# Late weights split in short pieces, a norm's statistics on ScalarE, and redrawn orders of work: one Trainium2 core

## The chip, the cores and the metric

The kernel runs on one core of a Trainium2 chip (trn2). A core has TensorE (PE; its weight loads are listed apart as PEld), VectorE (DVE), ScalarE (ACT), GpSimd (POOL) and SyncE (SP), which issues the transfers here. Each engine runs its own instruction stream in order, and they meet only at semaphores. The metric is device time in microseconds (us) of one launch: 243.81 us is the median of three runs before the change (243.23 to 246.11).

## The reference, cut to what matters

`x` is (4, 256, 256): four batches of 256 tokens with 256 channels, a condition vector per batch, all in float32. Two layers follow each other. The first has an adaptive LayerNorm, attention over 16 heads of 16 channels, a projection, a second adaptive norm and a MLP of 1024 hidden units; the second has a norm by the root mean square, attention over four heads of 64 channels, an output projection and a skip.

```python
# layer 0; sc, sh and gm are six vectors of silu(cond) @ Wada.T + bada
a = ln(x) * (1 + sc1) + sh1            # ln: (x - m) / sqrt(var + 1e-6)
q, k, v = a @ Wqkv.T                   # q and k scaled to unit norm per head
x2 = x + gm1 * (softmax(q @ k.T + bias) @ v @ Wproj.T + bproj)
b = ln(x2) * (1 + sc2) + sh2
x3 = x2 + gm2 * (gelu(b @ Wfc1.T + bfc1) @ Wfc2.T + bfc2)
# layer 1
c = x3 * (scale * rsqrt(mean(x3 ** 2) + 1e-6))   # scale comes from cond
q, k, v = c @ qkv_w.T                  # unit norm times sqrt(scale), then rope
out = x3 + softmax(q @ k.T + mask) @ v @ out_w.T
```

The three norms are called kinds 0, 1 and 2 below: `ln(x)`, `ln(x2)` and the one by root mean square of `x3`.

## The kernel before, in words

**Orders written by hand.** The work is cut into steps with a name, a batch and a part (`fc1:2.1` is part 1 of `fc1` for batch 2). Five lists at the file's head, SYNC_ORDER, TENSOR_ORDER, VECTOR_ORDER, SCALAR_ORDER and POOL_ORDER, say in which order each engine walks its share of the steps; the same name in two lists is that step's work on two engines. Semaphores carry the data dependences, and nothing else sets the order.

**TensorE and its buffers.** Results go to three PSUM banks named `ring`, claimed in the order of TENSOR_ORDER; each must be emptied by VectorE or ScalarE before its next claim. The attention scores have two buffers `psx`, the value products `pv`. A float32 matmul is taken as three products of high and low halves (L835 to L837), so each operand, weight or tile, is split: the high half is a rounded copy, the low half the difference. `busy` steps (L974) are filler matmuls between the others, two per unit, 33 units. `normed` steps transpose a normalised tile (L841), `turn1` rotated q and k, `fc1` and `fc2` are the MLP, `qk1` and `v1` the second layer's projections, `max0` the scores from which VectorE takes row maxima (L1223), `score0` those that ScalarE exponentiates (L620).

**A norm** of a batch is a chain through the engines: the step `stats` on VectorE takes two variance statistics and two aggregates (L1188, L1190), then adds epsilon (L1192 for kinds 0 and 1; L1195 and L1196 for kind 2, where the squared mean is added to the variance as well); `stats` on GpSimd raises to the power −0.5 (L482); VectorE normalises two tiles (L1206); TensorE transposes them; ScalarE modulates (L607, L610); VectorE splits (L1215, L1216).

**The unit norms** of q and k: `square1` on ScalarE (L677; L670 in the first layer), sums and a seed on VectorE (`rsums1`, L1417 to L1183), three Newton rounds on GpSimd (`root1`, L490 to L493), rope and a product on VectorE (L1434 to L1443; in the first layer the product is L1356), then the transposes `turn1`.

**The late weights** w1, w2, wqkv1 and wout1 are loaded by SyncE (L446 to L458) into two staging areas, their high halves are taken by ScalarE (L591), their low halves by GpSimd in one instruction each (L546, L550, L554, L558). GpSimd also makes the additive mask (L515), the square roots of the second layer's scales (`key_scales`, L581 and L582), bias terms (`xbias0`, L533 and L534; `xbias1`, L540 and L542) and half of the rope (`cos`, L574). SyncE moves the row shifts of the first attention (`shift0`, L437).

After `fc2` VectorE forms x3 (L1405, L1408), from which the third norm starts. The GELU tiles are split by ScalarE (L746) and VectorE (L1397), the attention output by L1263.

## Time and profile before

| | |
|---|---|
| median of three runs | 243.81 us (243.23 to 246.11) |
| the profiled execution, its own time | 244.3 us |
| its span, first to last instruction | 242.4 us |
| TensorE busy; weight loads | 228.3 us (94%); 175.6 us (72%) |
| VectorE busy | 201.6 us (83%), 418 instructions |
| ScalarE busy | 156.6 us (65%), 316 instructions |
| GpSimd busy | 95.3 us (39%), 167 instructions |
| mean granted TensorE clock, as a share of the full one | 0.983 |

The profile is one execution. Its span is 1.9 us below its own time, and that time is 0.5 above the median of the runs. A busy share is an average over stages; matmuls overlap, so a group's "mean ns" is the latency of one and not the distance to the next. In a timeline row the first number is the start within the span, the second the time that the row's instructions took, and the bracket says how long the engine had been idle before and what it waited for.

### The profile page before, as it was taken

What the parts mean: (1) busy time and instruction counts of PE and PEld (TensorE: products, weight loads), DVE (VectorE), ACT (ScalarE), POOL (GpSimd) and SP (SyncE); (2) the same over time, 40 slices, a digit from 0 to 9 for tenths busy, and PEclk for the clock granted to TensorE, in tenths of its full rate; (3) what the DMA queues carried; (4) which work ended last, traced back from release to release, by engine and by line L of the source; (5) the groups of instructions that cost most, each with busy time, mean ns of one, the idle gap of its engine ahead of it and who ended that gap; (6) DMA issues with size and microseconds to landing.
All of it is one profiled execution on the core that took longest, in us unless ns stands there. A gap on an engine that the chain in (4) does not pass through costs nothing.

```text
span 242.4 us, 4991 instructions
## 1 busy us (share of the span) xinstructions
PE 228.3 (94%) x1792; PEld 175.6 (72%) x1792; DVE 201.6 (83%) x418; ACT 156.6 (65%) x316; POOL 95.3 (39%) x167
## 2 busy tenths in 40 slices
PE   6999999999999999999999999999999799998982
PEld 2679674575567758567689999999897476867762
DVE  3879889999996997997977998776898988998743
ACT  2430491854899987985989828753608695877930
POOL 7416317028203302380839194234505545550000
PEclk9797999999999999999999999999999999999998
DMA  6970040000000003203000100000000000000112
GB/s 209 329 302 3 1 173 1 3 1 5 3 0 9 0 3 96 85 0 105 34 3 0 47 0 0 3 0 3 0 0 4 0 0 1 3 0 0 47 43 92
DMA packets 3641, 9.75 MB, mean 40 GB/s; under 512 B 536, under 2 KB 920, under 8 KB 3360
## 3 DMA queue, kind: packets, MB, share of 16 engines
q1 hardware_dynamic: 3616, 9.41, 11.3%
q8 instruction: 16, 0.26, 0.4%
q14 instruction: 9, 0.07, 0.1%
HBM read 8.23 MB, written 1.05 MB: 38 GB/s over the span
## 4 chain that ended last, share of the span: by engine, by line
PE 65%; DVE 15%; ACT 6%; issue 5%; POOL 3%; DMA 3%; SPq 1%; POOLq 0%; ACTq 0%; DVEq 0%
PE ring L835 11%; PE ring L841 10%; PE ring L836 10%; PE ring L837 10%; PE pv L944 5%; DVE nm L1223 5%; PE psx L974 5%; PE ring L898 3%; PE pv L1133 2%; PE psx L924 2%; DVE qn L1356 2%; DMA stage_a<-in_wada 2%; PE ring L848 1%; PE psx L1105 1%; DVE qstk L1397 1%
## 5 line engine op out<-in xcount | busy, mean ns | idle before, releaser
L1223 DVE TENSOR_REDUCE nm<-ring 128x2 f32<-128x512 f32 x64 | 40.2, 684 | 1.3 <-PE ring L898 0.8
L620 ACT ACTIVATE ps<-psx 128x1024 f32<-128x1024 f32 x32 | 31.4, 1026 | 6.0 <-PE psx L924 5.9
L835 PE MATMUL ring<-wqkv_hi,xm_hi 128*128 128x512 f32 (+1 forms) x64 | 24.2, 379 | 0.2
L974 PE MATMUL psx<-ident_b 128*128 128x512 bf16 x66 | 21.4, 449 | 2.0 <-POOL ones L477 2.0
L836 PE MATMUL ring<-wqkv_lo,xm_hi 128*128 128x512 f32 (+1 forms) x64 | 22.0, 343 | 0.0
L837 PE MATMUL ring<-wqkv_hi,xm_lo 128*128 128x512 f32 (+1 forms) x64 | 22.0, 343 | 0.0
L898 PE MATMUL ring<-kstk,qstk 64*128 64x256 f32 x128 | 19.4, 327 | 1.9 <-DVE nm L1223 1.6
L734 ACT ACTIVATE ps<-ring,col 128x256 f32<-128x256 f32 x32 | 13.3, 476 | 11.8 <-PE ring L837 11.2
L898 PEld LDWEIGHTS ring<-kstk,qstk 64*128 64x128 f32 x128 | 12.3, 184 | 10.5 <-DVE nm L1223 5.9
L490 POOL TENSOR_TENSOR nt<-ss,rn 128x64 f32<-128x64 f32 (+1 forms) x24 | 7.1, 296 | 32.3 <-DVE rn L1183 31.1
L574 POOL TENSOR_TENSOR stage_a<-qk,rope_sb 128x512 f32<-128x512 f32 x8 | 11.3, 1408 | 19.9 <-ACT qk L757 19.8
L835 PE MATMUL ring<-xm_hi,w_sb 128*128 128x256 f32 x64 | 18.5, 289 | 0.0
L836 PE MATMUL ring<-xm_lo,w_sb 128*128 128x256 f32 x64 | 18.1, 282 | 0.0
L837 PE MATMUL ring<-xm_hi,w_sb 128*128 128x256 f32 x64 | 18.1, 282 | 0.0
L944 PE MATMUL pv<-ps,vs 128*32 128x256 f32 x256 | 16.9, 385 | 0.0
L841 PE MATMUL ring<-ident,stack 128*128 128x128 f32 x128 | 16.0, 276 | 0.0
L841 PEld LDWEIGHTS ring<-ident,stack 128*128 128x128 f32 x128 | 14.2, 141 | 2.0 <-DVE nm L1223 0.4
L783 ACT ACTIVATE ps<-psx,nm 128x256 f32<-128x256 f32 x32 | 14.8, 484 | 1.1 <-DVE nm L1450 1.1
L542 POOL TENSOR_TENSOR xs<-x,stage_a 128x512 f32<-128x512 f32 x4 | 5.5, 1384 | 24.5 <-DVE x L1390 24.4
L482 POOL TENSOR_TENSOR rstd<-ve,half_neg 128x2 f32<-128x2 f32 x12 | 10.1, 844 | 12.2 <-DVE ve L1192 9.5
L835 PEld LDWEIGHTS ring<-wqkv_hi,xm_hi 128*128 128x128 f32 x64 | 12.6, 197 | 3.1 <-issue 0.7
L924 PE MATMUL psx<-qstk,kstk 64*128 64x256 f32 x128 | 13.6, 304 | 0.5 <-DMA qstk<-stage_a 0.2
(198 smaller groups left out, 680.2 us busy)
## 6 DMA issues: line engine op xcount, KB each, us to landing
stage_a<-in_wada SPq DMA_DIRECT2D x3, 512.0 KB, 8.5
xs<-in_x SPq DMA_DIRECT2D x4, 256.0 KB, 7.4
stage_a<-in_wfc SPq DMA_DIRECT2D x1, 1024.0 KB, 4.8
stage_b<-in_wfc SPq DMA_DIRECT2D x1, 1024.0 KB, 4.7
out<-x SPq DMA_DIRECT2D x4, 256.0 KB, 2.0
stage_b<-in_wqkv SPq DMA_DIRECT2D x1, 768.0 KB, 6.1
stage_a<-in_wqkv SPq DMA_DIRECT2D x1, 768.0 KB, 4.3
row<-in_rows SPq DMA_DIRECT2D x1, 394.0 KB, 8.0
```

Source lines behind the costliest of these rows:

```text
L620: a.activation(ps[:, n % 4], psx[:, n % 2], ACT.Exp).then_inc(exp_done, 1)
L734: last = a.activation(gelu_u[:, n % 4, i * L:(i + 1) * L], bank(key)[:, i * L:(i + 1) * L], ACT.Gelu_apprx_tanh, bias=col[:, 16 + 2 * i_ + ...
L783: ins = a.activation(weights_q[m % 2][:, i, f, :], psx[:, n % 2, i, f, :], ACT.Exp, bias=nm1[:, m % 2, 2 * i + f:2 * i + f + 1], accum_out ...
L835: mm(dst, lhs[0], rhs[0], start=start, stop=False)
L836: mm(dst, lhs[0], rhs[1], start=False, stop=False)
L837: return mm(dst, lhs[1], rhs[0], start=False, stop=stop)
L841: last = nc.tensor.transpose(dst[:, i * P:(i + 1) * P], src, ident[:, :])
L898: last = mm(dst[par][:, qc * L:(qc + 1) * L], qstk[rows_, b % 2, p, qc * P:(qc + 1) * P], kstk[rows_, b % 2, p, :], start=True, stop=not w ...
L924: last = mm(dst[:, i, kc, :], kstk[head_rows(i), b % 2, p, keys], qstk[head_rows(i), b % 2, p, :], start=True, stop=not with_bias)
L944: last = mm(pv[32 * i:32 * i + 32, cols_], vs[:, b % 3, kc, 4 * g + i, :], ps[:, slot, i % 2, kc, :], start=(kc == 0), stop=(kc == TB - 1))
L974: mm(psx[:, 0, 0], ident_b[:, :], ident_b[:, :].unsqueeze(1).to_broadcast([P, 4, P]), start=True, stop=True)
L1223: v.tensor_reduce(nm[:, :, par, p], bank(key).rearrange("p (q n) -> p q n", q=TB), AX.X, ALU.max, negate=True).then_inc(ring_dve, 1)
```

## The change

Four things change.

1. A function `take_lo` on GpSimd makes the low half of a late weight in pieces of 512 columns (4, 4, 3 and 1 of them) where one instruction did it. Only the last piece signals.
2. For kinds 0 and 1 VectorE no longer adds epsilon. `rstd_of` on GpSimd does it in an instruction of its own ahead of the power.
3. For kind 2 VectorE has no `stats2` step. ScalarE squares each of the batch's two tiles of x3 and sums it in the same instruction, each waiting for the one before; GpSimd multiplies the sum by 1/256 and adds epsilon.
4. The five lists are redrawn. SyncE issues w1's load behind the first row shift and w2's behind the fourth. GpSimd makes the key scales later and the bias term `xbias1:3` behind `root1:0`. TensorE keeps its 33 filler units, one more of them ahead of `ada`.

The file is longer by some lines, so line numbers differ: the statistics' squares are L696, the modulation L620, the q and k copy L778, the turned copy L793, the pieces L507, epsilon L487 and L490, the power L491.

On GpSimd, after the third batch's inverse root of the first attention (`rn` is the root, `sqs` the key scales), before and after:

```order
L493 TENSOR_TENSOR rn<-rn,nt 128x64
L524 TENSOR_TENSOR rn<-rn,sm 128x2x16
L581 TENSOR_TENSOR sqs<-row,half_pos 128x4
L582 TENSOR_TENSOR sqs<-row,half_pos 128x4
L515 TENSOR_SCALAR mask_add<-o_tok 128x2048
```

```order
L501 TENSOR_SCALAR nt<-nt 128x64
L502 TENSOR_TENSOR rn<-rn,nt 128x64
L539 TENSOR_TENSOR rn<-rn,sm 128x2x16
L530 TENSOR_SCALAR mask_add<-o_tok 128x2048
L499 TENSOR_TENSOR nt<-ss,rn 128x64
```

The two powers are gone from here, so the mask follows the root at once. In the same engine's stretch around the second MLP weight (`kstk` holds its low half), first before and then after:

```order
L540 TENSOR_TENSOR stage_a<-gam,row 128x256
L542 TENSOR_TENSOR xs<-x,stage_a 128x512
L533 TENSOR_TENSOR stage_a<-gam,row 128x256
L534 TENSOR_TENSOR xs<-xs,stage_a 128x512
L550 TENSOR_TENSOR kstk<-stage_b,kstk 128x2048
L482 TENSOR_TENSOR rstd<-ve,half_neg 128x2
L554 TENSOR_TENSOR wqkv_lo<-stage_a,wqkv_hi 128x1536
```

```order
L594 TENSOR_TENSOR sqs<-row,half_pos 128x4
L595 TENSOR_TENSOR sqs<-row,half_pos 128x4
L548 TENSOR_TENSOR stage_a<-gam,row 128x256
L549 TENSOR_TENSOR xs<-xs,stage_a 128x512
L507 TENSOR_TENSOR kstk<-stage_b,kstk 128x512 x4
L487 TENSOR_SCALAR ve<-mv 128x2
L491 TENSOR_TENSOR rstd<-ve,half_neg 128x2
L487 TENSOR_SCALAR ve<-mv 128x2
L491 TENSOR_TENSOR rstd<-ve,half_neg 128x2
L507 TENSOR_TENSOR wqkv_lo<-stage_a,wqkv_hi 128x512 x3
```

The key scales left the place ahead of the mask and stand ahead of w2's split; two norms' epsilon and power now come between the two splits, where one power stood.

On ScalarE, where the fourth batch's `fc2` ends and the second layer's attention begins (`junk` is the squares' unused output, `gam` and `vs` hold turned and value tiles), before and after:

```order
L762 ACTIVATE vs<-ring 128x2x256
L607 ACTIVATE xmt<-ring,mod 128x256 x4
L757 ACTIVATE qk<-ring 128x512
L772 ACTIVATE gam<-ring 128x4x128
L677 ACTIVATE qn<-qk 128x512
L757 ACTIVATE qk<-ring 128x512
L772 ACTIVATE gam<-ring 128x4x128
L677 ACTIVATE qn<-qk 128x512
```

```order
L783 ACTIVATE vs<-ring 128x2x256
L696 ACTIVATE junk,mv<-xs 128x256 x2
L620 ACTIVATE xmt<-ring,mod 128x256 x2
L793 ACTIVATE gam<-ring 128x4x128
L620 ACTIVATE xmt<-ring,mod 128x256 x2
L696 ACTIVATE junk,mv<-xs 128x256 x2
L793 ACTIVATE gam<-ring 128x4x128
L778 ACTIVATE qk<-ring 128x512
L690 ACTIVATE qn<-qk 128x512
L778 ACTIVATE qk<-ring 128x512
L690 ACTIVATE qn<-qk 128x512
```

The two pairs of squares are `stats2:2` and `stats2:3`. The second pair stands ahead of the second turned tile and of the next tile's copy and square.

The diff, with the lists of TensorE, VectorE and ScalarE cut to the head and the passage from the fourth batch's `fc2` on:

```diff
--- before.py
+++ after.py
@@ -67,6 +67,7 @@
 R_END = 1300
 R_KZERO = C
 FILL = 2
+PIECE = 512
 
 
 
@@ -81,80 +82,81 @@
 
 
 SYNC_ORDER = steps("""
-load_w1 shift0:0 shift0:1 shift0:2 load_w2 shift0:3 load_wqkv1 load_wout1 proj1:0 proj1:1 proj1:2 proj1:3
+shift0:0 load_w1 shift0:1 shift0:2 shift0:3 load_w2 load_wqkv1 load_wout1 proj1:0 proj1:1 proj1:2 proj1:3
 """)
 
 TENSOR_ORDER = steps("""
-busy:0 busy:1 busy:2 busy:3 busy:4 ada normed0:0 busy:5 busy:6 busy:7 busy:8 busy:9 busy:10 busy:11 qk0:0.0
...
-normed1:1 score0:3.6 score0:3.7 out0:3.0 proj0:2 value0:3.2 value0:3.3 fc1:0.0 fc1:0.1 fc1:0.2 out0:3.1 fc1:0.3
-heads0:3 fc1:1.0 fc1:1.1 proj0:3 normed1:2 fc1:1.2 fc2:0 fc1:1.3 fc1:2.0 fc1:2.1 normed1:3 fc1:2.2 fc1:2.3
-normed2:0 fc2:1 qk1:0.0 fc1:3.0 qk1:0.1 fc1:3.1 fc2:2 fc1:3.2 fc1:3.3 v1:0 normed2:1 fc2:3 normed2:2 qk1:1.0
...
+busy:0 busy:1 busy:2 busy:3 busy:4 busy:5 ada busy:6 normed0:0 busy:7 busy:8 busy:9 busy:10 busy:11 busy:12
...
+out0:3.1 fc1:0.3 heads0:3 fc1:1.0 fc1:1.1 fc1:1.2 proj0:3 fc1:1.3 normed1:2 fc2:0 fc1:2.0 fc1:2.1 fc1:2.2
+normed1:3 fc1:2.3 normed2:0 fc2:1 qk1:0.0 qk1:0.1 fc1:3.0 fc1:3.1 fc1:3.2 fc1:3.3 fc2:2 v1:0 normed2:1 turn1:0.0
+fc2:3 normed2:2 turn1:0.1 qk1:1.0 qk1:1.1 score1:0.0 score1:0.1 v1:1 normed2:3 qk1:2.0 qk1:2.1 v1:2 turn1:1.0
...
 score1:3.0 turnp1:2.1 turninv1:2 score1:3.1 value1:2 turnp1:3.0 proj1:1 turnp1:3.1 turninv1:3 value1:3 proj1:2
 proj1:3
 """)
 
 VECTOR_ORDER = steps("""
...
 unit0:3.1 v0:2 max0:2.4 max0:2.5 max0:2.6 lo0:3.0 max0:2.7 neg0:2 heads0_lo:0 lo0:3.1 shift0:2 proj0:0 stats1:0
 out0:1.0 max0:3.0 max0:3.1 max0:3.2 norm1:0 max0:3.3 max0:3.4 max0:3.5 out0:1.1 max0:3.6 max0:3.7 neg0:3
...
-fc2:1 stats2:1 gelu:2.3 gelu:3.0 rsums1:0 norm2:1 gelu:3.1 fc2:2 stats2:2 gelu:3.2 gelu:3.3 rope:0.0 split2:1
-norm2:2 rope:0.1 fc2:3 split2:2 stats2:3 rsums1:1 max1:0.0 norm2:3 max1:0.1 rope:1.0 rope:1.1 inv1:0.0 split2:3
-inv1:0.1 rsums1:2 max1:1.0 turnp1:0.0 turnp1:0.1 rope:2.0 rope:2.1 inv1:1.0 max1:1.1 rsums1:3 turnp1:1.0
...
+rsums1:0 norm2:1 gelu:2.3 gelu:3.0 gelu:3.1 gelu:3.2 rope:0.0 fc2:2 gelu:3.3 split2:1 rope:0.1 norm2:2 fc2:3
+split2:2 norm2:3 rsums1:1 max1:0.0 max1:0.1 rope:1.0 rope:1.1 split2:3 inv1:0.0 inv1:0.1 turnp1:0.0 rsums1:2
+turnp1:0.1 max1:1.0 rope:2.0 rope:2.1 heads1_scaled:0 inv1:1.0 max1:1.1 rsums1:3 max1:2.0 inv1:1.1 turnp1:1.0
...
 """)
 
 SCALAR_ORDER = steps("""
...
-gelu:3.0 gelu:3.1 fc1:3.2 gelu:3.2 fc1:3.3 gelu:3.3 v1:0 normed2:1 normed2:2 qk1:1.0 turn1:0.0 square1:1.0
-qk1:1.1 turn1:0.1 square1:1.1 v1:1 exp1:0.0 normed2:3 qk1:2.0 exp1:0.1 turn1:1.0 qk1:2.1 v1:2 turn1:1.1
...
+gelu:3.0 gelu:3.1 fc1:3.2 gelu:3.2 fc1:3.3 gelu:3.3 v1:0 stats2:2 normed2:1 turn1:0.0 normed2:2 stats2:3
+turn1:0.1 qk1:1.0 square1:1.0 qk1:1.1 square1:1.1 exp1:0.0 v1:1 normed2:3 exp1:0.1 qk1:2.0 qk1:2.1 v1:2
...
 """)
 
 POOL_ORDER = steps("""
-const_stack const_v stats0:0 const_sel stats0:1 stats0:2 root0:0 stats0:3 xbias0:0 root0:1 root0:2 key_scales
-mask root0:3 xbias1:0 xbias0:1 stats1:0 split_w1 xbias1:1 stats1:1 xbias0:2 xbias1:2 xbias0:3 split_w2 stats1:2
-split_wqkv1 xbias1:3 stats1:3 stats2:0 split_wout1 cos:0.0 cos:0.1 stats2:1 root1:0 stats2:2 cos:1.0 cos:1.1
-stats2:3 root1:1 cos:2.0 cos:2.1 root1:2 cos:3.0 cos:3.1 root1:3
+const_v const_sel stats0:0 stats0:1 stats0:2 root0:0 stats0:3 const_stack xbias0:0 root0:1 root0:2 mask root0:3
+stats1:0 xbias1:0 xbias0:1 split_w1 xbias1:1 stats1:1 xbias0:2 xbias1:2 key_scales xbias0:3 split_w2 stats1:2
+stats1:3 split_wqkv1 stats2:0 split_wout1 cos:0.0 cos:0.1 stats2:1 root1:0 xbias1:3 stats2:2 stats2:3 cos:1.0
+cos:1.1 root1:1 cos:2.0 cos:2.1 root1:2 cos:3.0 cos:3.1 root1:3
 """)
 
 BRANCH = TENSOR_ORDER.index(("branch",))
@@ -238,7 +240,8 @@
 
 def build(nc, x, wqkv, wproj, wada, wfc1, wfc2, wnorm, wqkv1, wout1, cols, rows, rope, bias, mask, out):
     ring_plan = Ring(TENSOR_ORDER)
-    stat_no = positions(VECTOR_ORDER, ["stats0", "stats1", "stats2"])
+    stat_no = positions(VECTOR_ORDER, ["stats0", "stats1"])
+    rstd_no = positions(POOL_ORDER, ["stats0", "stats1", "stats2"])
     norm_keys = [key[1:] for key in ring_plan.keys if key[0] == "xT"]
     norm_no = {key: n for n, key in enumerate(norm_keys)}
 
@@ -292,6 +295,7 @@
         mv = sb("mv", [P, 3, B, TB, 2])
         ve = sb("ve", [P, 3, B, TB])
         rstd = sb("rstd", [P, 3, B, TB])
+        junk = sb("junk", [P, C])
         zero_col = sb("zero_col", [P, 1])
         ss = sb("ss", [P, TB, 2 * H0])
         rn = sb("rn", [P, TB, 2 * H0])
@@ -358,7 +362,7 @@
         w_hi, w_lo_d, w_lo_p = sem("weights_hi"), sem("weights_lo_vector"), sem("weights_lo_pool")
         xb_ready = sem("x_bias_ready")
         x2_ready, x2b_ready, x3_ready = sem("x2_ready"), sem("x2_bias_ready"), sem("x3_ready")
-        stats_ready, rstd_ready = sem("stats_ready"), sem("rstd_ready")
+        stats_ready, rstd_ready, squares_summed = sem("stats_ready"), sem("rstd_ready"), sem("squares_summed")
         xh_ready, xmt_ready, xm_ready = sem("xh_ready"), sem("xmt_ready"), sem("xm_ready")
         sq_ready, seed_ready, rn_ready = sem("sq_ready"), sem("seed_ready"), sem("rn_ready")
         qn_ready, stk_hi, stk_lo = sem("qn_ready"), sem("stack_hi"), sem("stack_lo")
@@ -478,7 +482,12 @@
             g.memset(row[:, R_KZERO:R_KZERO + C], 0.0).then_inc(kbias_zero, 1)
 
             def rstd_of(kind, b):
-                pool.wait_ge(stats_ready, stat_no[(kind, b)] + 1)
+                if kind < 2:
+                    pool.wait_ge(stats_ready, stat_no[(kind, b)] + 1)
+                    step(g.tensor_scalar(ve[:, kind, b, :], mv[:, kind, b, :, 1], LN_EPS, None, ALU.add))
+                else:
+                    pool.wait_ge(squares_summed, TB * (b + 1))
+                    step(g.tensor_scalar(ve[:, kind, b, :], mv[:, kind, b, :, 1], 1.0 / C, LN_EPS, ALU.mult, ALU.add))
                 g.tensor_tensor(rstd[:, kind, b, :], ve[:, kind, b, :], half_neg[:, 0:TB], ALU.pow)\
                  .then_inc(rstd_ready, 1)
 
@@ -491,6 +500,12 @@
                     step(g.tensor_tensor(t, t, y, ALU.mult))
                     step(g.tensor_scalar(t, t, -0.5, 1.5, ALU.mult, ALU.add))
                     step(g.tensor_tensor(y, y, t, ALU.mult))
+
+            def take_lo(lo, whole, hi):
+
+                for n in range(0, whole.shape[1], PIECE):
+                    ins = g.tensor_tensor(lo[:, n:n + PIECE], whole[:, n:n + PIECE], hi[:, n:n + PIECE], ALU.subtract)
+                ins.then_inc(w_lo_p, 1)
 
             for step_ in POOL_ORDER:
                 name, b = step_[0], step_[1] if len(step_) > 1 else None
@@ -543,20 +558,18 @@
                                     ALU.add).then_inc(x2b_ready, 1)
                 if name == "split_w1":
                     pool.wait_ge(w_hi, 4)
-                    g.tensor_tensor(w1_lo, stage_a[:, 0:FC * HID].rearrange("p (f n) -> p f n", f=FC),
-                                    w1_hi, ALU.subtract).then_inc(w_lo_p, 1)
+                    take_lo(w1_sb[:, 1, :], stage_a[:, 0:FC * HID], w1_sb[:, 0, :])
                 if name == "split_w2":
                     pool.wait_ge(w_hi, 5)
-                    g.tensor_tensor(w2_lo, stage_b[:, :].rearrange("p (f n) -> p f n", f=HC),
-                                    w2_hi, ALU.subtract).then_inc(w_lo_p, 1)
+                    take_lo(w2_lo.rearrange("p f n -> p (f n)"), stage_b[:, :], w2_hi.rearrange("p f n -> p (f n)"))
                 if name == "split_wqkv1":
                     pool.wait_ge(w_hi, 6)
-                    g.tensor_tensor(wqkv_lo[:, :, :], stage_a[:, 0:FC * 3 * C].rearrange("p (f n) -> p f n", f=FC),
-                                    wqkv_hi[:, :, :], ALU.subtract).then_inc(w_lo_p, 1)
+                    take_lo(wqkv_lo[:, :, :].rearrange("p f n -> p (f n)"), stage_a[:, 0:FC * 3 * C],
+                            wqkv_hi[:, :, :].rearrange("p f n -> p (f n)"))
                 if name == "split_wout1":
                     pool.wait_ge(w_hi, 7)
-                    g.tensor_tensor(wo_lo[:, :, :], stage_b[:, 0:FC * C].rearrange("p (f n) -> p f n", f=FC),
-                                    wo_hi[:, :, :], ALU.subtract).then_inc(w_lo_p, 1)
+                    take_lo(wo_lo[:, :, :].rearrange("p f n -> p (f n)"), stage_b[:, 0:FC * C],
+                            wo_hi[:, :, :].rearrange("p f n -> p (f n)"))
                 if name == "root1":
                     inverse_root(seed1_ready, b, 2 * H1)
                     g.tensor_tensor(rn[:, :, 0:2 * H1], rn[:, :, 0:2 * H1],
@@ -675,6 +688,14 @@
                         act.wait_ge(*full(("T1", t - TB)))
                     act.wait_ge(*emptied(("qk1", t)))
                     a.activation(qn[:, t % TB, :], qk[:, t % TB, :], ACT.Square).then_inc(sq1_ready, 1)
+                if name == "stats2":
+                    act.wait_ge(x3_ready, b + 1)
+                    for i in range(TB):
+                        if b or i:
+                            act.wait_ge(squares_summed, TB * b + i)
+                        a.activation(junk[:, :], xs[:, TB * b + i, :], ACT.Square,
+                                           accum_out=mv[:, 2, b, i, 1:2])\
+                         .then_inc(squares_summed, 1)
                 if name == "hi0":
 
                     t = TB * b + i_
@@ -1187,18 +1208,14 @@
                 for i in range(TB):
                     step(v.bn_stats(bnst[:, kind, b, i, :], src[:, TB * b + i, :]))
                 for i in range(TB):
-                    step(v.bn_aggr(mv[:, kind, b, i, :], bnst[:, kind, b, i, :]))
-                if kind < 2:
-                    v.tensor_scalar(ve[:, kind, b, :], mv[:, kind, b, :, 1], LN_EPS, None, ALU.add).then_inc(stats_ready, 1)
-                else:
-
-                    step(v.tensor_tensor(ve[:, kind, b, :], mv[:, kind, b, :, 0], mv[:, kind, b, :, 0], ALU.mult))
-                    v.scalar_tensor_tensor(ve[:, kind, b, :], ve[:, kind, b, :], LN_EPS, mv[:, kind, b, :, 1],
-                                           ALU.add, ALU.add).then_inc(stats_ready, 1)
+                    last = v.bn_aggr(mv[:, kind, b, i, :], bnst[:, kind, b, i, :])
+                    if i == 0:
+                        step(last)
+                last.then_inc(stats_ready, 1)
 
             def normalise(kind, b, src):
                 n = norm_no[(kind, b)]
-                dve.wait_ge(rstd_ready, stat_no[(kind, b)] + 1)
+                dve.wait_ge(rstd_ready, rstd_no[(kind, b)] + 1)
                 if n >= 1:
                     dve.wait_ge(*full(("xT",) + norm_at[n - 1]))
                 for i in range(TB):
@@ -1406,9 +1423,6 @@
                      .then_inc(ring_dve, 1)
                     dve.wait_ge(*emptied(("f2", b)))
                     v.tensor_tensor(xs[:, batch, :], x2[:, batch, :], xs[:, batch, :], ALU.add).then_inc(x3_ready, 1)
-                if name == "stats2":
-                    dve.wait_ge(x3_ready, b + 1)
-                    statistics(2, b, xs)
                 if name == "rsums1":
                     if b >= 1:
                         dve.wait_ge(rn1_ready, b)
```

## Rows read from the trace of the kernel before

**Rows 1.** Stretches: from:to, length, busy of PE, PEld, DVE, ACT, POOL, clock, DMA, GB/s.

```profile
135.00:175.00 40.00, 39.36 (x317) 38.64 (x317) 32.58 (x66) 24.06 (x51) 18.48 (x23) 1.00 0.01 5
...
190.00:219.50 29.50, 27.59 (x192) 20.56 (x192) 26.51 (x51) 22.56 (x67) 14.68 (x35) 1.00 0.00 1
```

**Rows 2.** Waits of TensorE, whole span: engine, buffer, line, releaser: us, times, longest.

```profile
PE ring L841 <- DVE qn L1443: 1.8, 2, 1.2
PE ring L898 <- DVE nm L1223: 1.6, 6, 0.4
...
PE ring L835 <- DVE stack L1397: 0.5, 1, 0.5
```

**Rows 3.** Timeline, 58 to 64 us: start, us, engine, line, operation; idle before.

```profile
58.22 1.03 POOL L581 TENSOR_TENSOR sqs<-row,half_pos 128x4 f32<-128x4 f32 x1
...
58.80 0.68 DVE L1356 TENSOR_TENSOR qn<-qk,rn 128x512 f32<-128x512 f32 x1
...
60.44 1.90 POOL L515 TENSOR_SCALAR mask_add<-o_tok 128x2048 bf16<-128x2048 uint8 x1
60.60 2.27 DVE L1356 TENSOR_TENSOR qn<-qk,rn 128x512 f32<-128x512 f32 x1
```

**Rows 4.** Timeline, 125 to 138 us: w2's split and the GELU low parts.

```profile
128.69 4.60 POOL L550 TENSOR_TENSOR kstk<-stage_b,kstk 128x2048 fp32r<-128x2048 f32 x1
...
131.06 3.38 DVE L1397 TENSOR_TENSOR qstk<-ps,qstk 128x512 fp32r<-128x512 f32 x2 [0.17 <-ACT qstk L746]
...
135.10 0.38 PE L835 MATMUL ring<-wp_hi,at_hi 128*128 128x256 f32 x1 [0.30 <-DVE at_lo L1263]
```

**Rows 5.** Timeline, 139.5 to 143.3 us: the split of wqkv1 and an epsilon.

```profile
139.75 3.52 POOL L554 TENSOR_TENSOR wqkv_lo<-stage_a,wqkv_hi 128x1536 fp32r<-128x1536 f32 x1 [5.34 <-ACT wqkv_hi L591]
...
140.94 2.35 DVE L1192 TENSOR_SCALAR ve<-mv 128x2 f32<-128x2 f32 x1
```

**Rows 6.** Timeline, 180 to 194 us: x3, statistics, squares and the rope wait.

```profile
181.11 0.47 PE L835 MATMUL ring<-wqkv_hi,xm_hi 128*128 128x512 f32 x1
...
181.68 0.69 DVE L1408 TENSOR_TENSOR xs<-x,xs 128x512 f32<-128x512 f32 x1
...
182.58 0.60 PE L841 MATMUL ring<-ident,qn 128*128 128x128 f32 x4
...
183.35 0.88 DVE L1188 BATCH_NORM_STATS2 bnst<-xs 128x6 f32<-128x256 f32 x2
...
183.80 0.63 ACT L677 ACTIVATE qn<-qk 128x512 f32<-128x512 f32 x1
...
184.90 0.16 DVE L1196 SCALAR_TENSOR_TENSOR ve<-ve,mv 128x2 f32<-128x2 f32 x1
...
193.19 0.66 PE L841 MATMUL ring<-ident,qn 128*128 128x128 f32 x4 [1.17 <-DVE qn L1443]
```

**Rows 7.** Groups of VectorE: line, shapes, count; busy us, mean ns; idle before.

```profile
L1192 DVE TENSOR_SCALAR ve<-mv 128x2 f32<-128x2 f32 x8 | 4.2, 520 | 0.3
```

**Rows 8.** Groups of GpSimd: additions, the power, a Newton step, wout1's split.

```profile
L482 POOL TENSOR_TENSOR rstd<-ve,half_neg 128x2 f32<-128x2 f32 x12 | 10.1, 844 | 12.2 <-DVE ve L1192 9.5 <-DVE ve L1196 2.8
...
L534 POOL TENSOR_TENSOR xs<-xs,stage_a 128x512 f32<-128x512 f32 x4 | 5.1, 1282 | 0.3
...
L492 POOL TENSOR_SCALAR nt<-nt 128x16 f32<-128x16 f32 x12 | 3.2, 270 | 1.0
...
L558 POOL TENSOR_TENSOR wo_lo<-stage_b,wo_hi 128x512 fp32r<-128x512 f32 x1 | 1.8, 1822 | 5.1 <-ACT wo_hi L591 5.1
```

**Rows 9.** Groups of ScalarE: the exponential with sum and its read-out.

```profile
L783 ACT ACTIVATE ps<-psx,nm 128x256 f32<-128x256 f32 x32 | 14.8, 484 | 1.1 <-DVE nm L1450 1.1
...
L783 ACT ACTIVATION_READ_ACCUMULATOR ps<-psx,nm 128x1 f32 x32 | 6.9, 217 | 0.0
```

**Rows 10.** Timeline of SyncE, 30 to 140 us, and the page's transfer of w2.

```profile
110.61 1.27 SPq L437 DMA_DIRECT2D qstk<-stage_a  x2
...
stage_b<-in_wfc SPq DMA_DIRECT2D x1, 1024.0 KB, 4.7
```

89 lines of the change are left out of this document (45 added, 44 removed).

## The prediction

> **What bounds the kernel now.** Read the stretches first [rows 1]. From 135 to 175 us TensorE is busy 39.36 of 40.00 us at the full clock: in that stretch nothing that another engine does can shorten the run by more than 0.6 us. From 190 to 219.5 it is busy 27.59 of 29.50. So the question is not how busy VectorE is, but which of TensorE's few waits goes and which new one comes. The table of waits comes second [rows 2]: VectorE's rope product 1.8 us in two pieces, its row maxima of the first attention 1.6 in six, one GELU low part 0.5. VectorE's and GpSimd's work costs time only where it reaches such a wait.
>
> Third, the timeline, for what makes VectorE late. A VectorE instruction that meets a long GpSimd instruction lasts until that one ends. The unit-norm product takes 2.27 us beside the mask, against 0.68 just before [rows 3]; two GELU low parts take 3.38 beside the 4.60 us split of the second MLP weight [rows 4]; an addition of two columns takes 2.35, from 140.94 to 143.29, inside a split that ends at 143.27 [rows 5]. Over their usual lengths (0.68 each, and 0.16 for an operation on two columns, [rows 6]) that is 1.59 + 2.02 + 2.19 = 5.8 us.
>
> **The change part by part.**
>
> *Epsilon to GpSimd.* Eight VectorE additions go, 4.2 us of busy time [rows 7], of which 2.9 is more than the 0.16 that each needs. On GpSimd each becomes an instruction of about 270 ns in front of the power (the nearest row has 16 columns, [rows 8]): +0.1 us on a norm's chain, in all eight chains 0.8, all beside other work but the first at the head. I take 0, up to +0.2. The Trainium skill, "GPSIMD Engine Reference", section "When to use GPSIMD", gives plain elementwise work to VectorE as the faster engine, which speaks against this move; 270 against 160 ns agrees.
>
> *Weights in pieces.* The four splits have 2048, 2048, 1536 and 512 columns and now run as 4 + 4 + 3 + 1 pieces. The nearest row for a piece with two full inputs is GpSimd's 128x512 addition, 1282 ns; the upper one is the split that has 512 columns already, 1822 [rows 8]. Four pieces last 5.1 us by the first and 7.3 by the second, against 4.60 in one instruction; I take 5.1, which lies nearer to the 4.60. VectorE's longest wait shrinks towards one piece; the sum of its waiting need not. The Trainium skill, "SBUF — State Buffer", says in its section on who interferes with whom that VectorE and GpSimd hold a shared port for a whole instruction. The trace agrees: the 2.35 us addition ended with the split. By that rule alone the pieces would give 0 where four VectorE instructions follow each other. The place where it reaches TensorE is the 0.30 wait for a projection's low part at 135.10, behind the 3.38 us pair [rows 4]; I count that wait below, with the lists, and the pieces themselves 0.
>
> On the other side stands the w2 split's start. The key-scale powers, from 58.22 to 60.44 [rows 3], moved ahead of it: 128.69 + 2.2 = 130.9. With pieces of 1.28 it ends at 136.0, with 1.82 at 138.2. Behind it on GpSimd is the next norm's epsilon and power (0.27 + 0.84, [rows 8]), then VectorE normalises two tiles of 256 columns, 0.7 if each takes half of the 0.68 that 512 take: the tile is there at 137.8 or at 140.0. TensorE wanted it one projection unit after 135.10. Such a unit is twelve products of 256 columns, and six of 512 took 182.58 − 181.11 = 1.47 [rows 6], so at 136.6; two further `fc1` units of that length now come first: 139.5. So 1.7 us to spare, or 0.5 late: 0, up to +0.5. The split of wqkv1 now waits behind the fourth batch's epsilon too, whose projection moved one `fc1` unit back; it ended at 143.27 [rows 5], and between the tile at 139.5 and `qk1:0.0` TensorE has two `fc2` and five `fc1` units, 7.4 us by the latter alone: 0.
>
> *Third norm to ScalarE.* VectorE loses four times 1.71 us (183.35 to 185.06, [rows 6]), 6.8 us. ScalarE gets eight squares of 256 columns with a summed output. The nearest rows are its exponential of that width with sum: 484 ns, and 217 for the read-out [rows 9]. I take 0.65 each because every square waits for the one before; 0.48 and 0.70 are the ends. That is 1.3 per batch (0.97 to 1.4), 5.2 in all. Batches 0 to 2 stand in stretches with room, ScalarE 24.06 busy of 40 [rows 1]: 0. Batch 3 is the place to watch, in the rivals.
>
> *Mask and key scales.* The mask moves 2.2 us ahead, to 58.2, where VectorE runs maxima rather than the product that was held for 1.59. Since TensorE waits for those maxima 0.4 at most at a time [rows 2], I take −0.4, between 0 and −1.5.
>
> *Loads.* w2's load goes to behind the fourth shift (110.61 + 1.27 = 111.9) and lands 4.7 us later [rows 10], 12 us before GpSimd's split of it: 0. Without that cover the split and the 0.5 us margin behind it would go at once. w1's load, behind the first shift, has more room still.
>
> *Redrawn lists.* TensorE keeps its 33 filler units. At the head one more stands before the conditioning products, and the first data come by DMA either way: −0.2 (−0.2 to 0). ScalarE squares the second batch's last q and k tile ahead of a copy of about 0.6 instead of behind it, and a root on GpSimd follows: −0.4 (−0.6 to 0). The six maxima waits lose some in the stretch to 135: −0.2 (−1.0 to 0). The GELU wait of 0.5 before `fc2:3` [rows 2]: TensorE now has the four transposes of `turn1:0.0` first, 0.6 by the row at 182.58 [rows 6], while VectorE splits the last GELU tile later, behind `fc2:2`. With the 0.30 of 135.10: −0.5 together (−0.8 to +0.4). At 193.19 TensorE waits 1.17 for the rope product; ahead of that transpose stand now two more units, `qk1:2.1` and `v1:2`, of 1.47 each. All of it would go, less what batch 3's squares take from the same chain: −0.6 (−1.17 to +1.3).
>
> Sum: 0 + 0 + 0 − 0.4 − 0.2 − 0.4 − 0.2 − 0.5 − 0.6 = −2.3. The profiled execution took 244.3, so 242.0; the median of the runs shown, 243.81, lies 0.5 under it: **241.5 us**.
>
> **The rivals.**
> *ScalarE becomes the wait (slower).* `stats2:3` must wait for the sum x3, which VectorE ends at 182.37, and stands now ahead of a copy of turned tiles, the next tile's copy and its square; that square began at 183.80 [rows 6]. Now it can begin at 182.37 + 1.3 + two copies of 0.6 = 184.9, 1.1 later, and root, rope and the transpose of 193.19 follow. If the three ring banks hold back the two units meant as cover, the 1.17 wait grows to 2.3 while the other terms give nothing: 243.8 + 1.1 to 1.3 = 245.0, and 245.7 with the 0.5 and 0.2 above. It decides from the point where the square begins over 2.4 us after x3 (1.4 before) and the wait at this transpose stays above 1. For it: ScalarE executes in order. Against: VectorE, which held the chain as well, is 1.7 us freer at just this place.
>
> *Nothing moves.* TensorE is dense, and each removed wait is followed by another as long: 243.8, within 1 us. For it: 39.36 of 40.
>
> *VectorE was the bound all along (faster).* 11 us of its work go and up to 5.8 of port waits could follow. If all that the bounds name goes (0.2 + 0.6 + 1.5 + 1.0 + 0.8 + 1.17 = 5.3), the time is 238.5. For it: the large waits of TensorE are all for VectorE [rows 2]. Against: they are spread over a dozen places, and behind each stands a TensorE with other work.
>
> **How the numbers follow.** Forecast, a gain of 1 to 4.9: 0.57. Nothing moves: 0.21. ScalarE's wait, or another that ends above 244.8: 0.12. VectorE the bound: 0.10. Two per cent is 4.9 us, which is about what a measurement of this kernel, its three runs 2.9 us apart, tells from no change. Under 238.9 lie the last rival and a little of the forecast: faster 0.12. Over 248.7 lies only a loss in a place not named here: 0.04. The range goes from 238.5, that rival's value, to 245.4, within the slow rival's; the forecast's own is 239.5 to 243.
>
> **What would show it.** VectorE's busy sum some 11 us lower, ScalarE's 5 higher; no VectorE instruction held for over 1.5 us beside a split; the unit-norm product at 0.68 everywhere; the rope wait of TensorE gone in the stretch from 185; the last squares' successor within 2.4 us of x3. Wrong if TensorE's total waiting stays as it was, if pieces cost 1.8 us each, or if TensorE waits for the tile behind the w2 split.

## The result: slower by 1.25 %, and the profile after

The changed kernel took 248.06 us (median of 19 runs, 244.93 to 249.58) against 243.75 for the kernel before (median of 19); the ratio is 1.0125 with a 95% interval of 1.0094 to 1.0157. The ratio leaves out the four longest of the 19 runs as slow ones, so it is smaller than the 4.3 us (1.8%) between the medians. The prediction was 241.5. The runs of the changed kernel stand in two groups: eight have spans of 243.1 to 244.9 us and ten of 246.2 to 247.7, with one between. The kernel before has two levels as well, 16 runs of 242.5 to 244.6 us and three of 246.0 to 246.7; front_only below shows that they are another matter. The profile shown first is of the lower group, 245.02 us with a span of 243.2; a second profile of the same kernel, `after_again`, is of the upper one, span 246.8.

The page after, lower group: busy times, and TensorE's granted clock in 40 slices.

```profile
PE 228.3 (94%) x1792; PEld 174.5 (72%) x1792; DVE 193.6 (80%) x386; ACT 160.2 (66%) x332; POOL 100.5 (41%) x187
...
PEclk9999999999999999999999999999999989999999
```

VectorE lost 8 us of busy time instead of the 11 forecast, ScalarE gained 3.6 instead of 5, and GpSimd gained 5. TensorE's work is the same to 0.1 us. So the result is once more a matter of its waits. The table of them answers to [rows 2] (engine, buffer, line, releaser: us in total, times, longest):

```profile
PE ring L862 <- ACT qk L778: 1.9, 1, 1.9
...
PE ring L856 <- ACT vs L783: 1.4, 1, 1.4
PE ring L919 <- DVE nm L1240: 1.3, 4, 0.4
PE ring L856 <- ACT ps L755: 0.8, 1, 0.8
PE ring L856 <- DVE at_lo L1280: 0.6, 1, 0.6
```

Of the three waits of before, rope's 1.8 and the GELU part's 0.5 are gone as table entries, and the maxima's 1.6 fell to 1.3. In their place TensorE waits 1.9, 1.4 and 0.8 for **ScalarE to empty a ring bank**, for which it had not waited over 0.2 us before. The stretches that answer to [rows 1]:

```profile
135.00:175.00 40.00, 39.20 (x314) 38.16 (x313) 27.30 (x48) 24.18 (x58) 20.03 (x30) 1.00 0.02 7
190.00:219.50 29.50, 26.19 (x176) 18.98 (x176) 24.12 (x47) 21.58 (x64) 14.17 (x36) 0.94 0.01 2
```

From 135 to 175 VectorE has 5.3 us less to do than before and TensorE is no busier. From 190 to 219.5 TensorE is busy 1.4 us less, and the granted clock was 0.94 on average, where the profile before has 1.00 in that stretch.

Three sums of TensorE's waits (those over 0.05 us) tell where the time came and went; later kernels are put beside them. The last row is the kernel of load_order, the changed one but for two loads, whose profile (span 246.2) is of the upper group too.

| profile | 30 to 124 us | 124 to 183 (MLP) | 183 to 223 (second layer) | granted 1.2 GHz for 3.4 us at |
|---|---|---|---|---|
| before | 3.23 | 0.83 | 2.33 | 8.9, 19.1 |
| changed, lower group | 2.56 | 1.42 | 3.31 | 198.4 |
| changed, upper group | 2.53 | 3.93 | 3.33 | 146.6, 201.2 |
| load_order, upper group | 2.51 | 3.00 | 4.44 | 146.7 |

**The second layer.** The timeline of the changed kernel (start, us, engine; the bracket says how long the engine was idle and for whom), which answers to [rows 6]:

```profile
183.22 2.55 POOL L587 TENSOR_TENSOR stage_a<-qk,rope_sb 128x512 f32<-128x512 f32 x2
...
183.27 2.65 DVE L1223 TENSOR_SCALAR xh<-xs,zero_col,rstd 128x256 f32<-128x256 f32 x2 [1.12 <-POOL rstd L491]
...
185.84 1.26 DVE L1431 TENSOR_REDUCE ss<-qn 128x8 f32<-128x512 f32 x2
...
191.36 0.50 PE L856 MATMUL ring<-wqkv_hi,xm_hi 128*128 128x512 f32 x1 [1.36 <-ACT vs L783]
...
192.48 0.69 DVE L1457 TENSOR_TENSOR qn<-qn,rn 128x512 f32<-128x512 f32 x1 [1.08 <-POOL rn L575]
...
194.43 1.27 POOL L587 TENSOR_TENSOR stage_a<-qk,rope_sb 128x512 f32<-128x512 f32 x1 [2.05 <-ACT qk L778]
...
194.60 1.64 DVE L1457 TENSOR_TENSOR qn<-qn,rn 128x512 f32<-128x512 f32 x1
...
196.28 0.60 ACT L778 ACTIVATE qk<-ring 128x512 f32<-128x512 f32 x1 [1.92 <-DVE qn L1457]
...
197.02 0.63 PE L862 MATMUL ring<-ident,qn 128*128 128x128 f32 x4 [1.89 <-ACT qk L778]
```

VectorE's two normalising operations meet the two `cos` products of GpSimd and take 2.65 us instead of 0.74 before. Two moves bring them together: GpSimd's list now has that norm's power (`stats2:3`) ahead of the `cos` pair instead of behind it, and VectorE's list has the normalising pair ahead of the row sums. So the row sums start at 185.84, although their squares were ready at 185.07. The root (`rn`), which before ended while VectorE had other work, now ends so late that VectorE itself waits for it (1.08 before the product at 192.48). TensorE cannot use `qk1:2.1` and `v1:2` freely as cover meanwhile. `qk1:2.1` itself waits 1.36 us, because the ring bank of `v1:1` is not emptied: ScalarE has that behind `exp1:0.0`. Then the transpose `turn1:1.1` needs the bank of `qk1:2.1`, whose copy overwrites a buffer that rope must have read. That copy waits 1.92 for the rope product (itself held to 1.64 us by the next `cos`), and TensorE waits 1.89 for the copy.

**The MLP, upper group.** The timeline of `after_again`:

```profile
140.71 1.71 DVE L1223 TENSOR_SCALAR xh<-x,mv,rstd 128x256 f32<-128x256 f32 x2 [0.61 <-POOL rstd L491]
...
140.83 4.12 POOL L507 TENSOR_TENSOR wqkv_lo<-stage_a,wqkv_hi 128x512 fp32r<-128x512 f32 x3 [0.15 <-ACT wqkv_hi L604]
...
142.34 1.49 DVE L1232 CAST xm_hi<-xmt 128x512 fp32r<-128x512 f32 x1
...
143.87 1.63 DVE L1233 TENSOR_TENSOR xm_lo<-xmt,xm_hi 128x512 fp32r<-128x512 f32 x1
...
145.56 0.39 PE L856 MATMUL ring<-xm_hi,w_sb 128*128 128x256 f32 x1 [2.63 <-DVE xm_lo L1233]
```

and of the lower group at the same place:

```profile
141.11 0.42 DVE L1232 CAST xm_hi<-xmt 128x512 fp32r<-128x512 f32 x1
...
141.56 0.69 DVE L1233 TENSOR_TENSOR xm_lo<-xmt,xm_hi 128x512 fp32r<-128x512 f32 x1
...
142.03 4.78 POOL L507 TENSOR_TENSOR wqkv_lo<-stage_a,wqkv_hi 128x512 fp32r<-128x512 f32 x3 [1.61 <-ACT wqkv_hi L604]
```

In the profile of the upper group the three pieces of wqkv1's split and three VectorE instructions in a row take turns: the second normalising operation, the cast and the low part are held to 1.71 (for two), 1.49 and 1.63 us, and the tile that `fc1:2.0` needs is there at 145.5 instead of 142.25. TensorE waits 2.63 us. In the profile of the lower group GpSimd comes to that split 1.2 us later, when the chain is through. The profiles of load_order and turn_order, both of the upper group, show the same: the split at 140.9 and TensorE's wait of 2.63 or 2.64. Behind this wait the clock falls (stretch, length, busy of PE, PEld, DVE, ACT, POOL, granted clock, DMA):

```profile
143.20:146.60 3.40, 1.04 (x8) 1.05 (x9) 3.37 (x4) 0.00 (x0) 1.75 (x2) 1.00 0.00 0
146.60:150.01 3.41, 3.41 (x18) 3.41 (x17) 1.40 (x3) 1.74 (x6) 0.36 (x2) 0.50 0.00 0
150.01:153.40 3.39, 3.39 (x31) 3.39 (x30) 0.74 (x2) 2.58 (x7) 0.53 (x1) 1.00 0.00 0
```

TensorE was busy 1.04 of 3.40 us, and for the next 3.41 us it was granted 1.2 GHz instead of 2.4: 18 matmuls came where the stretch behind has 31. In the profile of the lower group such a stretch stands in the second layer, behind the 1.36 and 1.89 us waits:

```profile
194.90:198.38 3.48, 1.59 (x15) 1.26 (x12) 2.52 (x5) 2.10 (x5) 2.23 (x2) 1.00 0.01 2
198.38:201.79 3.41, 3.41 (x14) 1.74 (x13) 2.40 (x6) 1.78 (x4) 0.50 (x3) 0.50 0.00 0
```

How much each costs can be read by matching TensorE's matmuls one by one, load_order's profile against that of the lower group. It is 0.4 us ahead up to this wait, 2.5 behind right after it, 3.7 behind at the end of the stretch at 1.2 GHz, and 2.6 behind from 149.5 us on, where the lower group waits 0.78 for ScalarE. So the wait makes 2.9 us of the 3.1 between the groups, and of the 1.2 that the stretch costs about 1.0 comes back.

The Trainium skill, "SBUF — State Buffer", section on who interferes with whom, has it that the engine that issues first holds the shared port for its whole instruction. The alternation above agrees: each of VectorE's three instructions gives way to one piece of 1.3 to 1.5 us.

### The profile page after: what moved, and what is told of

Its sections match the earlier page's. It is cut to its first block, busy times and chain, and to the rows that moved or that the text cites. A ratio compares the mean times of both kernels' runs of the same rounds, so it can differ in the third digit from the quotient of the medians.

```text
span 243.2 us, 4998 instructions
## 1 busy us (share of the span) xinstructions
PE 228.3 (94%) x1792; PEld 174.5 (72%) x1792; DVE 193.6 (80%) x386; ACT 160.2 (66%) x332; POOL 100.5 (41%) x187
## 4 chain that ended last, share of the span: by engine, by line
PE 65%; DVE 19%; POOL 5%; issue 5%; ACT 3%; DMA 1%; SPq 0%; ACTq 0%; POOLq 0%; DVEq 0%
PE ring L862 13%; PE ring L856 9%; PE ring L858 7%; PE ring L857 7%; PE pv L965 5%; PE psx L995 5%; DVE nm L1240 5%; PE ring L919 4%; PE psx L945 3%; PE pv L1154 3%; PE psx L1126 3%; DVE qstk L1414 2%; DVE xh L1223 1%; DVE stack L1414 1%; DVE bnst L1209 1%
## 5 line engine op out<-in xcount | busy, mean ns | idle before, releaser
L856 PE MATMUL ring<-wqkv_hi,xm_hi 128*128 128x512 f32 (+1 forms) x64 | 23.5, 368 | 1.4 <-ACT vs L783 1.4
L995 PE MATMUL psx<-ident_b 128*128 128x512 bf16 x66 | 20.0, 427 | 2.0 <-POOL ones L481 2.0
L858 PE MATMUL ring<-wqkv_hi,xm_lo 128*128 128x512 f32 (+1 forms) x64 | 21.5, 337 | 0.0
L919 PE MATMUL ring<-kstk,qstk 64*128 64x256 f32 x128 | 18.4, 322 | 1.3 <-DVE nm L1240 1.3
L587 POOL TENSOR_TENSOR stage_a<-qk,rope_sb 128x512 f32<-128x512 f32 x8 | 10.4, 1313 | 14.1 <-ACT qk L778 14.1
L856 PEld LDWEIGHTS ring<-wqkv_hi,xm_hi 128*128 128x128 f32 x64 | 12.1, 189 | 5.1 <-ACT vs L783 1.8
L487 POOL TENSOR_SCALAR ve<-mv 128x2 f32<-128x2 f32 x8 | 2.9, 366 | 28.6 <-DVE mv L1211 28.3
L856 PEld LDWEIGHTS ring<-xm_hi,w_sb 128*128 128x128 f32 x64 | 12.2, 191 | 1.7 <-ACT ps L755 1.0
```

What stands on the lines that cost most here:

```text
L856: mm(dst, lhs[0], rhs[0], start=start, stop=False)
L858: return mm(dst, lhs[1], rhs[0], start=False, stop=stop)
L919: last = mm(dst[par][:, qc * L:(qc + 1) * L], qstk[rows_, b % 2, p, qc * P:(qc + 1) * P], kstk[rows_, b % 2, p, :], start=True, stop=not w ...
L995: mm(psx[:, 0, 0], ident_b[:, :], ident_b[:, :].unsqueeze(1).to_broadcast([P, 4, P]), start=True, stop=True)
```

## The experiments

Ratios are to the kernel before, run on the same chip, with a 95% interval. The chips differ from one set of runs to another, so kernels are compared by their ratios first.

**after_again**, no edit. 

> The changed kernel once more, nothing altered. Its 19 runs fell into two groups, spans of 243.1 to 244.0 us and of 246.2 to 247.7, at the same granted clock (0.992 and 0.993 in both groups). Theory 'two levels': again both groups occur, 3 us apart, and a trace of the higher one shows one place with 3 us more. Rival 'spread': spans fill the range between 243 and 247 evenly and no single place holds the difference.

247.09 us, 1.0124 (1.0073 to 1.0176). Five spans of 243.0 to 244.9, one of 245.7, four of 246.2 to 246.8. All three traces of the upper group (this one, load_order, turn_order) have the surplus at one place, above: 'two levels' holds in the main. This one has another 1.1 us at a GELU wait of 0.94 at 177 us, which the other two lack.

**turn_order**, TensorE and ScalarE:

```diff
-... v1:1 normed2:3 qk1:2.0 qk1:2.1 v1:2 turn1:1.0 ...
+... v1:1 normed2:3 qk1:2.0 turn1:1.0 qk1:2.1 v1:2 ...      # TensorE
-... exp1:0.0 v1:1 normed2:3 exp1:0.1 qk1:2.0 qk1:2.1 v1:2 turn1:1.0 ...
+... v1:1 exp1:0.0 normed2:3 exp1:0.1 qk1:2.0 turn1:1.0 qk1:2.1 v1:2 ...   # ScalarE
```

> The changed kernel, but turn1:1.0 stands ahead of qk1:2.1 and v1:2 again on TensorE and ScalarE, and v1:1 ahead of exp1:0.0 on ScalarE. Theory 'ring banks': in the changed kernel TensorE waits 1.36 us at 191.4 for ScalarE to empty v1:1 and 1.89 at 197.0 for the copy of qk1:2.1, which itself waits for rope; before, the waits of this place were 0.48, 1.17 and 0.61. So these two fall from 3.25 to about 1.7 and the span is 1 to 1.6 us shorter than the changed kernel's. Rival 'the rope chain decides': the 2.65 us of the two normalising operations beside the cos pair keep the root late, the waits only move to turn1:1.0, and the time stays within 0.5 us.

247.69 us, 1.0133 (1.0039 to 1.0228): nothing gained. The two waits became one of 3.22 us for rope:

```profile
185.93 2.66 DVE L1222 TENSOR_SCALAR xh<-xs,zero_col,rstd 128x256 f32<-128x256 f32 x2 [1.11 <-POOL rstd L490]
...
195.90 0.66 PE L861 MATMUL ring<-ident,qn 128*128 128x128 f32 x4 [3.22 <-DVE qn L1456]
```

The 2.66 us of the normalising pair beside `cos` are there as in the changed kernel, and between 183 and 223 us TensorE waits 4.59 us, against 4.44 in load_order's profile of the same group. So the rival holds: the banks decide on which instruction TensorE waits, the rope chain decides how long.

**load_order**, SyncE's list of before:

```diff
-shift0:0 load_w1 shift0:1 shift0:2 shift0:3 load_w2 ...
+load_w1 shift0:0 shift0:1 shift0:2 load_w2 shift0:3 ...
```

> The changed kernel with SyncE's order of before: w1's load ahead of the first row shift, w2's ahead of the fourth. Theory 'loads collide': the higher group of runs comes from the 1 MB loads that now follow the row shifts directly; the higher group disappears or is as rare as before (3 runs of 19). Rival 'loads are hidden': 12 us of cover, so both groups stay as frequent and the lower group stays at 243.1 to 244.0 us of span.

248.01 us, 1.0122 (1.0003 to 1.0241), three of four runs at 246.2 us of span or more and one at 243.3: both groups stay. Four runs can't tell how often each comes, but the loads are not what makes the upper one.

**code_only**: the three code parts with the lists of before (stats2 from VectorE's list to ScalarE's). 

> The kernel before with the three code parts of the change (pieces of 512, epsilon on GpSimd, squares on ScalarE), the lists of before, stats2 being moved to ScalarE's list at the same places and left out of VectorE's. Theory 'the redrawn lists cost it': the code parts alone are worth 0 to -1 us against before (243.4). Rival 'the parts cost it': pieces with 1.28 to 1.8 us each, epsilon on GpSimd and ScalarE's squares are themselves 1 to 3 us slower.

244.82 us, 1.0057 (1.0012 to 1.0101), 1.4 us slower: inside the rival's 1 to 3, and somewhat under half of the 3.0 by which the ratio puts the changed kernel behind. Three more kernels took one part each, in the lists of before.

**pieces_only**: `PIECE = 512` and `take_lo`. 

> The kernel before with pieces of 512 columns alone. code_only, with all three code parts, took 1.4 us more than before. Theory 'pieces': 3 pieces last 4.1 us against 3.5, 4 last up to 6.5 against 4.6 where VectorE takes turns with them; the norm behind comes later, +0.4 to +1.0 us. Rival 'pieces are neutral or good': the low part for the projection at 135 waits less, TensorE's waits at 148 and 152 don't appear, -0.3 to +0.2.

243.58 us, 0.9970 (0.9933 to 1.0007): no change that the ratio can tell. But nine of the 35 runs of the kernel before stood on its higher level here and one of these 14. Among the lower spans alone the medians are 241.05 before and 241.6 with pieces, half a microsecond longer; front_parts below bears this out.

**eps_only**:

```diff
+                if kind < 2:                                                    # GpSimd
+                    step(g.tensor_scalar(ve[:, kind, b, :], mv[:, kind, b, :, 1], LN_EPS, None, ALU.add))
...
-                    v.tensor_scalar(ve[:, kind, b, :], mv[:, kind, b, :, 1], LN_EPS, None, ALU.add).then_inc(stats_ready, 1)
+                    last.then_inc(stats_ready, 1)                               # VectorE
```

> The kernel before with the epsilon addition of the first two norms on GpSimd, nothing else. Theory 'chain': the addition on GpSimd takes 0.2 to 0.57 us against 0.17 on VectorE, in chains that are mostly covered: 0 to +0.3. Rival 'eps costs it': TensorE waits at the normed tiles near 134, 148 and 152, as in code_only (0.45, 0.40, 0.22): +0.6 to +1.0.

242.95 us, 0.9988 (0.9951 to 1.0026): neutral. In the changed kernel an epsilon took 366 ns in the mean against the 270 forecast, and w2's four pieces 6.0 us against 5.1 (line, shapes, count; busy us, mean ns; idle before):

```profile
L507 POOL TENSOR_TENSOR kstk<-stage_b,kstk 128x512 fp32r<-128x512 f32 x4 | 6.0, 1522 | 0.0
...
L487 POOL TENSOR_SCALAR ve<-mv 128x2 f32<-128x2 f32 x8 | 2.9, 366 | 28.6 <-DVE mv L1211 28.3
```

**squares_only**: `stats2` from VectorE to ScalarE. 

> The kernel before with the third norm's statistics as squares on ScalarE, at the places that code_only has them; pieces and epsilon as before. Theory 'ScalarE in order': the rope wait of TensorE near 193 grows from 1.17 to 1.6 as in code_only, nothing else: +0.3 to +0.6. Rival 'squares are free': VectorE's 1.7 us less at this place pays for it, -0.3 to +0.1.

244.78 us, 1.0057 (1.0012 to 1.0101): this part alone costs as much as the three together, as far as the intervals tell. The rope wait grew from 1.17 to 1.59, as expected, and there is a second, which neither theory named:

```profile
149.18 0.42 ACT L696 ACTIVATE junk<-xs 128x256 f32<-128x256 f32 x1
...
150.05 0.70 POOL L490 TENSOR_TENSOR rstd<-ve,half_neg 128x2 f32<-128x2 f32 x1
...
151.66 0.63 PE L862 MATMUL ring<-ident,xh 128*128 128x128 f32 x4 [0.82 <-DVE xh L1222]
```

ScalarE does the squares of batch 0 between `fc1` activations (the second one here), the power is done at 150.75, and TensorE waits 0.82 for the tile. Before, VectorE made these statistics in time. 0.82 + 0.42 is 1.24 of the 1.4 us. The sum of the parts is not the whole, though: in code_only this wait of 0.82 is 0.22, and waits of 0.45 and 0.40 stand at 134 and 148 us instead.

**split_first**, VectorE:

```diff
-... gelu:1.0 gelu:1.1 norm1:3 split1:2 gelu:1.2 ...
+... gelu:1.0 gelu:1.1 split1:2 norm1:3 gelu:1.2 ...
```

> The changed kernel with one step moved: split1:2 on VectorE stands ahead of norm1:3 again, as before the change. Theory 'collision': in the higher group of the changed kernel the three pieces of wqkv1's split (140.83 to 144.95) hold the normalising operation, the cast and the low part of that tile for 1.71, 1.49 and 1.63 us, TensorE waits 2.63 us at 145.6 and is granted 1.2 GHz from 146.6 to 150.0. With the split ahead, the higher group (246 to 247.7 of span) disappears and all runs stand at 243 to 244.5. Rival 'the clock's own lottery': the granted clock falls near 146 us in most runs whatever VectorE does, and both groups stay.

246.99 us, 1.0148 (1.0119 to 1.0177), five spans of 244.4 to 245.6. In these five runs the upper group is gone, as the theory says, but so is the lower. TensorE's waits:

```profile
PE ring L862 <- ACT qk L778: 1.9, 1, 1.9
...
PE ring L862 <- DVE qn L1457: 1.4, 2, 1.2
...
PE ring L856 <- DVE stack L1414: 0.9, 1, 0.9
PE ring L856 <- DVE x L1422: 0.9, 1, 0.9
```

The 2.63 wait is gone and two of 0.9 have come: with the tile through, the pieces hold the next VectorE instructions, the GELU low parts and the emptying of `fc2:0`'s bank. And with no stretch at 1.2 GHz near 198 us a wait of 1.19 for rope comes to light at 211, which the profiles with that stretch lack. Half of the theory holds.

**one_piece**, `PIECE = 2048`. 

> The changed kernel with each late weight split in one instruction (2048, 2048, 1536, 512 columns), as before the change; the lists stay. Theory 'order, not pieces': one instruction of 3.5 us from about 141 holds the same VectorE chain for as long as three pieces do, TensorE waits over 1.5 us at 145 in some runs, and both groups stay. Rival 'the pieces take turns': each of three VectorE instructions waits for a piece of its own only because there are pieces; with one instruction the chain is held once, ends over 1 us earlier, and the higher group goes.

247.25 us, 1.0165 (1.0138 to 1.0192), spans 245.0 to 246.0. No wait of 2.63, so the taking of turns does need the pieces; but the one instruction holds two GELU low parts for 5.28 us, and TensorE waits 1.71 for the projection's low part:

```profile
127.21 4.62 POOL L508 TENSOR_TENSOR kstk<-stage_b,kstk 128x2048 fp32r<-128x2048 f32 x1
...
127.70 5.28 DVE L1415 TENSOR_TENSOR qstk<-ps,qstk 128x512 fp32r<-128x512 f32 x2
...
134.84 0.38 PE L857 MATMUL ring<-wp_hi,at_hi 128*128 128x256 f32 x1 [1.71 <-DVE at_lo L1281]
```

In these lists pieces and no pieces cost about the same. The rival's 'over 1 us earlier' was not gained.

**pool_late**, GpSimd and VectorE:

```diff
-... root0:2 mask ... xbias1:2 key_scales xbias0:3 split_w2 stats1:2 stats1:3 split_wqkv1 ...
+... root0:2 key_scales mask ... xbias1:2 xbias0:3 split_w2 stats1:2 split_wqkv1 stats1:3 ...      # GpSimd
-... norm1:3 split1:2 gelu:1.2 gelu:1.3 fc2:0 ...
+... split1:2 gelu:1.2 gelu:1.3 fc2:0 norm1:3 ...      # VectorE
```

> The changed kernel with GpSimd's key_scales ahead of the mask and stats1:3 behind the split of wqkv1, as before the change, and on VectorE split1:2 ahead of norm1:3 and norm1:3 behind fc2:0, as before. Theory 'GpSimd's order between the splits': w2's split starts 2.2 us earlier and wqkv1's right behind it or beside the low parts only; TensorE's waits between 125 and 180 fall from 1.4 to 3.9 us to under 1.2, no run stands at 246 us of span or more, and the span is 0.5 to 1 us shorter than the lower group's 243.3. Rival 'VectorE is held anyway': twelve pieces take the same port time wherever they stand, the waits only move, and the span stays at 243.3 or above.

247.03 us, 1.0142 (1.0112 to 1.0172). The MLP's waits fell to 1.19 and none of four runs passed 245.5 us of span; but the mask in its old place holds the two unit-norm products again, for 2.98 us together instead of 1.28:

```profile
58.14 2.98 DVE L1373 TENSOR_TENSOR qn<-qk,rn 128x512 f32<-128x512 f32 x2
```

TensorE's matmuls, 0.2 us ahead of the changed kernel's profile up to there, stand 1.4 behind it afterwards, so the mask's place is worth 1.6 us. The second layer waited 4.23 instead of 3.31. Theory and rival both fail as put: what the MLP gained, the mask and the second layer took.

**no_squares**: `stats2` back on VectorE in the changed lists, behind each `fc2`; `norm2:3` behind `max1:0.0`, `norm2:0` behind `split1:3`. 

> The changed kernel with the third norm's statistics on VectorE again, stats2 behind each fc2, norm2:3 behind max1:0.0 and norm2:0 behind split1:3; pieces, epsilon and the lists else as changed. Theory 'squares cost 1.4 here too': the lower group goes from 243.3 to about 242, since the square of the next tile need not wait for stats2:3. Rival 'the order costs it': TensorE's waits of 1.36 and 1.89 stay, being set by the ring banks behind exp1 and rope, and the span stays within 0.5 us of 243.3.

254.26 us, 1.0436 (1.0407 to 1.0464): a miss. The edit put `norm2:0` behind a tile that is itself late; TensorE waits 2.63, 2.85 and 2.13 in the MLP, and behind each it is granted 1.2 GHz for 3.4 us (from 146.6, 156.8 and 184.2). It says nothing of the squares.

**no_squares_back**: the same with the second layer in the order of before. 

> As no_squares, and the second layer in the order of before in all lists behind the fourth batch's fc2 (turn1:0.0 stays where the change has it). Theory 'the new order costs it': TensorE's waits behind 182 us become those of before (0.48, 1.17, 0.61), 2.3 in all against 3.3 to 4.4, and the span is 1 to 2 us shorter than that of no_squares. Rival: the order there is worth under 0.4 us.

251.86 us, without an interval. It has two stretches at 1.2 GHz in the MLP and none behind, no_squares four in all, so the 2.4 us between the two are not the order's alone.

**front_only**: the kernel before, with the redrawn lists up to the last scores of the first attention. 

> The kernel before in all its code, with the redrawn lists up to the last scores of the first attention (score0:3.7 on TensorE and ScalarE, split1:0 on VectorE, stats1:1 on GpSimd), and the order of before behind that; SyncE's list as before. Theory 'front gains, back loses': in the changed kernel the first attention stood 1.6 us earlier at 120 us than in code_only, with nothing but the lists different there; that 1.6 stays, so 241.5 to 242.0 against 243.2 to 243.4 for the kernel before. Rival 'a gain in front is given back': the MLP is bound by VectorE's chain, the earlier start is eaten by longer waits at 135 to 175, and the time is that of before within 0.4 us.

241.72 us, **0.9928 (0.9900 to 0.9955)**, twelve spans of 239.5 to 240.4. It beats both kernels. Behind the front its waits are those of before to 0.02 us (0.83 and 2.32 in the table's stretches). Part of its gain is the higher level of the kernel before, which it doesn't have: of all runs of the kernel before, 27 of 124 stood some 3 us above the rest, of the 48 of front_only, front_parts, front_code and mended_2, which share the redrawn front, none. The one trace of that level, pieces_only's (span 245.4), is 2.5 us late by 16 us and still 2.5 at 121, so it arises at the head. Among the lower spans alone the medians are 241.05 and 239.8, a gain of 1.25 us. The waits:

```profile
PE ring L841 <- DVE qn L1443: 1.8, 2, 1.2
...
PE ring L835 <- DVE stack L1397: 0.5, 1, 0.5
```

**front_parts**: front_only with pieces and epsilon on GpSimd. 

> front_only with the pieces of 512 and the epsilon on GpSimd, no squares. Theory 'additive': pieces 0.997 and epsilon 0.999 multiply with 0.993: 240.7 to 241.2. Rival 'pieces and epsilon are nothing': 241.7 as front_only, within 0.2%.

242.37 us, 0.9950 (0.9923 to 0.9977): neither. The two parts do not add a gain, and by ratio and median they cost 0.5 to 0.65 us on front_only. TensorE's waits between 124 and 183 us are 1.44 instead of 0.83, with two that front_only lacks or has shorter (0.29 at the first place):

```profile
132.71 0.39 PE L842 MATMUL ring<-wp_hi,at_hi 128*128 128x256 f32 x1 [0.45 <-DVE at_lo L1272]
...
147.00 0.63 PE L848 MATMUL ring<-ident,xh 128*128 128x128 f32 x4 [0.40 <-DVE xh L1215]
```

**front_code**: all three code parts and the redrawn front, the order of before behind it. 

> All three code parts of the change and its lists up to the last scores of the first attention; the order of before behind that, with stats2 on ScalarE as in code_only; SyncE as before. Theory 'the late lists cost it': front_only (0.993) and code_only (1.0057) multiply to 0.9985, about 243.3, with no run at 246 us of span; the changed kernel's late lists then cost 1 % in the lower group and 2.5 % in the higher. Rival 'the parts collide with the front': the earlier front puts the pieces beside other work and the time is 245 or more with the order of before as well.

242.99 us, 0.9966 (0.9941 to 0.9991), spans 240.8 to 241.6. The product forecast 243.3. So by the ratios the late lists alone take the kernel from 0.9966 to 1.0125, 1.6 % or 3.9 us.

**mended_2**: the changed kernel with split_first's edit and the second layer in the order of before (ScalarE copies `turn1:0.0` ahead of `normed2:2`, as changed). 

> The changed kernel with split1:2 ahead of norm1:3 on VectorE and the order of before behind the fourth batch's fc2 on all engines, except that turn1:0.0 stays ahead of normed2:2 on ScalarE. Theory 'two places': these two account for the loss behind 124 us, 243.5 to 244.5 and no higher group. Rival 'the MLP's order as a whole': TensorE's waits of 0.9 to 1 us at 147, 175 or 182 stay, and the time is 245 or more.

243.97 us, 0.9993 (0.9957 to 1.0029), spans 241.1 to 242.9, no upper group. The second layer:

```profile
189.32 0.73 DVE L1222 TENSOR_SCALAR xh<-xs,zero_col,rstd 128x256 f32<-128x256 f32 x2
...
193.81 0.66 PE L861 MATMUL ring<-ident,qn 128*128 128x128 f32 x4 [1.59 <-DVE qn L1456]
```

With `cos` ahead of that norm's power on GpSimd, and the row sums and a maximum ahead of the normalising pair on VectorE, the pair misses `cos` and takes 0.73, and TensorE waits 1.59; its waits between 183 and 223 us are 2.74. By the ratios these two places are 3.2 us of the late lists' 3.9; the rest is the MLP's order, whose waits are 2.65 still. Two first forms (back_half, with the second layer's order alone, 246.15 us, and mended, 245.31) had ScalarE empty banks in another order than TensorE claims them, so part of their second layer is not computed from the right data; they are not used.

## Why the prediction was wrong, point by point

| step of the prediction | forecast, us | measured |
|---|---|---|
| head, second root, mask, maxima (front) | −1.2 | −1.75, front_only; −1.25 among the lower spans |
| epsilon on GpSimd | 0 | −0.3 ± 0.9, eps_only |
| pieces | 0 | −0.7 ± 0.9, pieces_only; +0.55 among the lower spans |
| pieces and epsilon together | 0 | +0.5 to +0.65, front_parts against front_only |
| squares on ScalarE | 0 | +1.4, squares_only |
| waits at `fc2:3` and 135 us | −0.5 | +0.7, what mended_2 leaves of the late lists |
| rope wait of the second layer, and `split1:2` | −0.6 and not seen | +3.2, mended_2 |

The last two rows go by ratios, in which both groups are mixed. The traces part them. Here is how much later (minus: earlier) TensorE starts the same matmul than in the profile before: the last score of the first attention, the last `fc2`, the last value product of the second layer.

| profile | at 121 us | at 181 us | at 234 us |
|---|---|---|---|
| front_only | −2.1 | −2.1 | −2.1 |
| front_code | −3.15 | −1.8 | −1.3 |
| changed, lower group | −2.8 | −1.3 | +1.1 |
| load_order, upper group | −3.0 | +1.3 | +4.1 |
| mended_2 | −2.35 | +0.55 | +0.6 |

Between the first two the lower group loses 1.5 us, of which front_code, with the order of before, loses 1.3 already: that is the price of the three parts. The upper group loses 4.4. Between the last two the changed kernel loses 2.3 and front_code 0.55; mended_2 loses nothing. So the second layer's new order costs about 1.8 us, the parts 1.9 over both stretches, and the collision of the upper group 2.9 more. Putting `split1:2` first takes that collision away at the price of 1.4 us against the lower group (mended_2 and split_first both lose 2.9 from 121 to 181 us). The first column depends on the head of each profile as well (front_only −0.9, front_code −2.0 and the lower group −1.7 at 31 us), so it is no measure of the lists alone.

**The front was right in its mechanism.** That its sum came out near is in part luck: the mask was worth more than the 0.4 taken, 1.25 us between the profiles of before and front_only. It now runs ahead of the two unit-norm products, which take 1.28 us together where one of them had taken 2.27 [rows 3]:

```profile
56.47 1.90 POOL L530 TENSOR_SCALAR mask_add<-o_tok 128x2048 bf16<-128x2048 uint8 x1
...
58.34 1.28 DVE L1373 TENSOR_TENSOR qn<-qk,rn 128x512 f32<-128x512 f32 x2
```

Putting it back cost 1.6 us (pool_late), just over the outer bound of 1.5. That the loads and the epsilon by itself cost nothing was right too, and the later split of w2 did not make its tile late by more than 0.36 us.

**The step that failed first** is "all of it would go" at 193.19, the −0.6 of the sum. In its place TensorE waits 1.36 and 1.89 us, its waits between 183 and 223 us are 3.31 instead of 2.33, and the second layer takes it 2.3 us longer than before. The prediction counted two units of TensorE's own work as cover for the rope product. A unit is cover only if a ring bank is free for it, and one bank was to be emptied by a copy that waits for that same rope product. The first rival named the banks, and turn_order shows that even without them the chain, not the cover, sets the wait. The rival's price of 245.0 was for 1.1 us more on the chain; the squares' start, 2.15 us behind x3, stayed under its mark of 2.4. The chain was late from another side: VectorE's normalising pair, redrawn ahead of the row sums, stood beside GpSimd's `cos`, redrawn behind the power that the pair waits for. The prediction looked for such waits only beside the mask and the splits. That the place is the second layer's order is shown by mended_2; that within it this meeting is the cause is read from the two timelines, since mended_2 moves other steps there too.

**The second** is the sentence on pieces. It held that the sum of VectorE's waiting need not shrink and then booked 0, having checked only the tile behind the w2 split and what follows the split of wqkv1. With the epsilon the pieces cost 0.5 us and more even in the order of before (front_parts). Beside w2's split two VectorE instructions were still held over 1.5 us (1.78 and 1.81). The new place of `split1:2`, behind `norm1:3` and so beside wqkv1's split, was not followed. Where three dependent VectorE instructions stand beside three pieces, each waits for a piece, and in the upper group this reached TensorE. By the traces the groups part 10 us earlier, at the projection's low part on VectorE beside the w2 split, in the lower group and then in `after_again`:

```profile
132.22 1.81 DVE L1280 TENSOR_TENSOR at_lo<-stage_a,at_hi 128x512 fp32r<-128x512 f32 x1
```

```profile
131.93 0.66 DVE L1280 TENSOR_TENSOR at_lo<-stage_a,at_hi 128x512 fp32r<-128x512 f32 x1
```

load_order and turn_order have 0.66 as well. The later tile of the lower group lets ScalarE's split of wqkv1, and GpSimd's behind it, begin 1.2 us later. That this decides it in every run was not tried.

**The third** is the squares' 0. ScalarE had room on average, 24.06 of 40, but in order it does not choose its time. A pair took 1.1 us, inside the forecast's 0.97 to 1.4:

```profile
L696 ACT ACTIVATE junk<-xs 128x256 f32<-128x256 f32 x8 | 3.3, 417 | 5.7 <-DVE xs L1425 5.6
...
L696 ACT ACTIVATION_READ_ACCUMULATOR junk<-xs 128x1 f32 x8 | 1.5, 187 | 0.0
```

The price was right and the place was wrong: in squares_only one norm's tile reached TensorE 0.82 us later and one rope product 0.42. What the squares cost within the redrawn lists is not known, since no_squares, the try at it, moved another step too.

**Not counted at all** was what a wait can cost on top: a stretch of 3.4 us at 1.2 GHz. One followed the wait of 2.63 us in five of the six profiles that have it (after_again, load_order, turn_order, no_squares and no_squares_back, but not back_half). Behind 1.36 and 1.89 in a row it came in the changed kernel's two profiles and in pool_late, but not in load_order, split_first and one_piece with the same two waits, nor behind turn_order's 3.22. So such a stretch is no fixed price of a wait. The net cost was small in both places where it can be read: 0.2 us in the MLP, above, and nothing in the second layer, below.

The rival 'VectorE was the bound' is out: its 8 us gave nothing where TensorE was dense. 'Nothing moves' is out as well: 1.25 to 1.75 us moved forward in front, and more moved back behind.

## What to carry to other kernels

An instruction stands as cover for a wait only if its own buffer is free without that wait: before counting on a reordered unit, follow who empties its bank, and what that copy waits for in turn. Where two engines hold each other up, as VectorE and GpSimd do here, look at which instructions a redrawn list puts beside each other: cutting the long one in pieces cannot help a chain of short ones, each of which waits for a piece. And price redrawn lists by halves: here the first half of the lists was worth −0.7 %, the code parts cost some 0.4 % on top of it and the second half of the lists 1.6 %, so a part of the change beat the whole. A kernel with two levels of time also needs its runs compared level by level: the pieces look neutral in one ratio and cost half a microsecond in another comparison.

## What the runs showed of the hardware

One program can run at two levels 3 us apart on the same chip, at the same mean granted clock (0.992 in runs with spans of 243.1 and 246.5). That clock says nothing of where the levels differ: the lower profile and load_order's upper one each have one stretch at 1.2 GHz, at 198.4 and at 146.7 us. But for 0.2 to 0.3 us from the head on, the traces part first where VectorE and GpSimd's pieces meet beside the w2 split, 10 us ahead of the wait.

And a stretch at 1.2 GHz may cost nothing. From 197 to 202 us it costs the lower profile 1.6 us against load_order's, which has none there; by 210 us load_order has lost 1.7 again, 1.19 of it in a wait for the rope product. split_first and one_piece, without the stretch, have that wait too (1.19 and 1.18); the changed kernel's two profiles, with it, do not, and pool_late, with it too, waits 0.83. So most or all of that wait is covered by the slower stretch.
